# A two-part transformer block on one core: query-score chunks moved up behind the key-score chunks of the same number

## The reference, cut to what matters

```python
scores = jnp.einsum('bqhd,bkhd->bhqk', Qh, Kh) / np.sqrt(dh)
scores = jnp.where(key_mask[:, None, None, :] == 0, NEG, scores)
scores = jnp.where(tril[None, None, :, :] == 0, NEG, scores)
attn = jax.nn.softmax(scores, axis=-1)
attn = attn * query_mask[:, None, :, None]
out = jnp.einsum('bhqk,bkhd->bqhd', attn, Vh).reshape(B, T, U)
out = out + x            # and a layer norm with gamma and beta behind it
```

## Time and profile before

| what | value |
|---|---|
| runs | 536.09, 537.47, 538.89 us; median 537.47 |
| profiled execution | 538.71 us, its span 536.9 us |
| mean granted clock of PE over the span | 0.942 |
| busy shares of the span | PE 83%, DVE 76%, ACT 59%, POOL 23% |
| attention stage, first key chunk | from 209.15 us |

### The profile page before, as it was taken

One profiled execution on the slowest core, in us unless ns is written; L12 is line 12 of the kernel. 1 busy time (PEld: TensorE's weight loads), 2 busy tenths in 40 slices (PEclk: granted clock), 3 DMA queues, 4 the chain that ended last, 5 costly groups with the idle time before them and its releaser, 6 DMA issues.

```text
span 536.9 us, 10757 instructions
## 1 busy us (share of the span) xinstructions
PE 447.4 (83%) x3773; PEld 275.3 (51%) x3773; DVE 406.4 (76%) x1008; ACT 315.3 (59%) x670; POOL 124.7 (23%) x345
## 2 busy tenths in 40 slices
PE   0049545988999739999999999999999999999981
PEld 0026334766777515565555555555556556556540
DVE  6898988887884238576977877877878878887715
ACT  0029135977888803566656666656667567566670
POOL 8000000000000011001045045045054063072181
PEclk9999958989999955799999999999999999999997
DMA  8900021223333351122122222322212213212000
GB/s 220 295 20 0 20 80 43 75 80 98 98 98 88 110 146 22 47 76 62 56 83 67 72 67 66 85 56 66 85 53 77 82 46 93 64 48 69 2 21 20
DMA packets 28585, 39.68 MB, mean 74 GB/s; under 512 B 5751, under 2 KB 19959, under 8 KB 28535
## 3 DMA queue, kind: packets, MB, share of 16 engines
q1 hardware_dynamic: 28486, 39.03, 26.0%
q10 hardware_dynamic: 48, 0.01, 0.0%
HBM read 25.91 MB, written 10.49 MB: 68 GB/s over the span
## 4 chain that ended last, share of the span: by engine, by line
PE 55%; DVE 6%; issue 1%; ACT 1%; DVEq 0%; ACTq 0%
PE banks L979 15%; PE banks L1010 14%; PE banks L998 13%; PE banks L981 6%; PE banks L1000 5%; DVE mx L837 3%; PE banks L1020 3%; DVE stats L879 1%; DVE aggr L883 1%; ACT pt L950 0%; ACT ots L934 0%; PE banks L988 0%; DVE res L866 0%; DVE res L869 0%; DVE mixed L870 0%
## 5 line engine op out<-in xcount | busy, mean ns | idle before, releaser
L837 DVE TENSOR_REDUCE mx<-banks 128x1 f32<-128x384 f32 (+3 forms) x384 | 212.5, 598 | 59.7 <-PE banks L981 52.5
L950 ACT ACTIVATE pt<-banks 128x512 f32<-128x512 f32 (+2 forms) x384 | 184.8, 528 | 110.4 <-PE banks L1000 104.1
L981 PE MATMUL banks<-causal,ident_b 128*128 128x128 bf16 x512 | 106.8, 228 | 0.0
L1000 PE MATMUL banks<-causalT,ident_b 128*128 128x128 bf16 x512 | 103.7, 222 | 0.0
L979 PE MATMUL banks<-w_room 73*128 73x512 bf16 (+3 forms) x256 | 75.3, 331 | 11.5 <-DVEq L912 10.3
L1010 PE MATMUL banks<-pt,vg 128*9 128x512 f32 (+3 forms) x1024 | 81.9, 438 | 0.5 <-ACT pt L950 0.5
L998 PE MATMUL banks<-w_room 76*128 76x512 bf16 (+3 forms) x256 | 71.2, 310 | 0.0
L979 PE MATMUL banks<-k_odd,q_odd 73*128 73x512 bf16 (+3 forms) x256 | 69.0, 302 | 1.6 <-DVE mx L837 1.6
L998 PE MATMUL banks<-q_odd,k_odd 76*128 76x512 bf16 (+3 forms) x256 | 67.6, 300 | 2.0 <-ACT pt L950 2.0
L750 POOL TENSOR_SCALAR mneg<-mx 128x16 f32<-128x16 f32 x32 | 8.1, 253 | 197.9 <-DVEq L845 197.9
L981 PEld LDWEIGHTS banks<-causal,ident_b 128*128 128x128 bf16 x512 | 52.1, 102 | 0.0
(11 more groups left out here) (155 smaller groups left out, 615.7 us busy)
## 6 DMA issues: line engine op xcount, KB each, us to landing
k_scratch<-parts SPq DMA_DIRECT2D x40, 128.0 KB, 2.3
w_room<-q_scratch SPq DMA_DIRECT2D x48, 96.0 KB
w_room<-k_scratch SPq DMA_DIRECT2D x48, 96.0 KB
q_odd<-q_scratch SPq DMA_DIRECT2D x48, 96.0 KB
k_odd<-k_scratch SPq DMA_DIRECT2D x48, 96.0 KB
q_scratch<-parts SPq DMA_DIRECT2D x24, 128.0 KB, 2.3
w_room<-in_w_dram SPq DMA_DIRECT2D x1, 2048.0 KB, 9.2
xn_all<-xn_st SPq DMA_DIRECT2D x8, 256.0 KB, 2.4
```

What stands on the lines that cost most here:

```text
L837: ins = dve.tensor_reduce(mx[:, u % 2, heads[0]:heads[-1] + 1, q], banks[:, S0 + c % RING, 0:w * len(heads)].rearrange("p (h k) -> p h k", ...
L950: act.activation(weights(k, heads[0], len(heads)), banks[:, ST0 + j % RING, 0:(T - P * k) * len(heads)], ACT.Exp, scale=SCALE).then_inc(ex ...
L981: ins = mm(o[:, w - P:w], ident_b[:, :], causal[:, :], start=False, stop=True)
L1000: ins = mm(o[:, 0:P], ident_b[:, :], causalT[:, :], start=False, stop=True)
```

## The change

Query chunk number j now stands directly behind key chunk number j, for all j. The short run of products V23 stands behind S2, not between K2 and S1, and the long run V01 stands behind S10, not ahead of it. The wait for the loads of the group g + 2 stays ahead of S0, so it now stands directly behind K0.

```diff
                         for j in range(NCH):
                             keys(tok, par, g, j)
+                            if ahead:
+                                if first and (g, j) == (2, 0):
+                                    pe.wait_ge(ones_in[1], 32)
+                                if j == 0:
+                                    loaded = stack_in[par if g + 2 < NG else 1 - par][(g + 2) % NG]
+                                    pe.wait_ge(loaded, tok.next(loaded, UNIT_DMAS))
+                                chunk(tok, par, g + 2, j)
                             if behind and j == 2:
                                 values(prev, 2)
                                 values(prev, 3)
                             if j == 10:
                                 values(g, 0)
                                 values(g, 1)
-                            for c in ((), (0,), (1,), (2, 3))[j] if j < 4 else (j,):
-                                if not ahead:
-                                    break
-                                if first and (g, c) == (2, 0):
-                                    pe.wait_ge(ones_in[1], 32)
-                                if c == 0:
-                                    loaded = stack_in[par if g + 2 < NG else 1 - par][(g + 2) % NG]
-                                    pe.wait_ge(loaded, tok.next(loaded, UNIT_DMAS))
-                                chunk(tok, par, g + 2, c)
                             if j == 3 and not (last and g == NG - 1):
                                 maxima(tok, g + 1)
```

## The result

The changed kernel takes 542.98 us in the median of five runs (541.76 to 543.19), the kernel before 536.78 us in five runs (536.09 to 538.89; the 537.47 from which the forecast started is the median of the first three). The ratio of the runs is 1.0096, 95% interval 1.0078 to 1.0114: about 1% or 5 us slower. The two medians alone are 6.2 us apart, 1.2%, a little more than that interval holds. The forecast was 543.1.

What follows compares the result with a forecast made beforehand. Bound: PE's own 9.40 us per plain group plus about 0.27 us of waits, ScalarE's 2.50 us run setting K7. Terms +6.1 - 0.4 = +5.7 us on the 537.47 median: 543.2, taken as 543.1; 8-in-10 range 540.0 to 546.5.

Steps and rivals of the forecast that it cites:

- (1): Query chunk S10 moved ahead of the long run V01: only moves VectorE's idle time, worth 0.
- (2): Ahead of K3: one more 512-column chunk, 2.53 us instead of 2.25, so K3 and ScalarE's run come 0.28 us later.
- (3): K3 to K7: ScalarE's 2.50 us stand, PE waits about 0.54 us, K7 at K0 + 5.03 instead of 4.75.
- (4): VectorE in plain groups: S6's 0.14 us wait goes, worth 0; group 9.95 us, +0.28 us 22 times, +6.1 us.
- (5): Groups where VectorE also makes the previous batch's statistics: 10.09 us instead of 10.15, -0.06 us 7 times, -0.4 us.
- (6): First group, at PE's low clock: PE's own work exceeds ScalarE's run, so 0, at most +0.1 us; last two groups 0.
- (7): Other engines' waits (copy L934, mask row, loads): all covered; uncovered, each would cost at most 0.28 us per group.
- Rival A: K7's 0.12 us wait comes from VectorE's delay of S6; PE's waits vanish, plain groups 9.40, 531.1 us; 6%.
- Rival B: K4's exponential is tied to transpose MX, not K3, so K7 stays at K0 + 4.75; no change, 537.1 us; 5%.
- Rival C: ScalarE's 0.25 us idle ahead of K4's exponential waits for K4, so K7 can follow K3 by 2.25; 537.8 us; 4%.
- Rival D: PE's clock grant falls in the regular 0.54 us wait, one group per batch at least 3.8 us longer; 573 us; 2%.
- Rival E: ScalarE's occasional delays come more often or a cover is missing: up to another 0.28 us per group, 549 us; 4%.

Runs made afterwards that it cites:

- the last experiment: Changed kernel with statistics moved, maxima copy behind K4's exponential, attended-rows copy behind K5's, OUT and its use one chunk later: 525.69 us, ratio 0.9793.

## Why the prediction was right, point by point

- What bounds: 9.40 us of PE's own work and two waits, one of them ScalarE's. Right; the last experiment measures 9.41, and the first two measures of K3 to K7, in the earlier trace rows, already said which wait was the floor.
- (1) S10 is worth 0: ratio 1.000 (0.9987 to 1.0014) alone.
- (2) K3 at K0 + 2.53: 2.52. MX at 3.08: 3.08.
- (3) PE waits 0.55 us ahead of K7 (0.54 expected) and K7 stands at 5.03: 327.17 less 322.14. The mechanism follows ScalarE's run one to one over three lengths.
- (4) VectorE waits less, S6 waits no more, and it is worth 0: so it is. The walk for VectorE had S0 to S2 at 0.76, 1.37 and 1.98 and S3 at 3.28; the row has three in one stretch from 0.87, and the fourth at 3.28. The start was missed by 0.11 us because S11 is reduced right ahead of S0 and the program waits there for its own reduction: 0.24 us idle, the same 0.24 that in most statistics groups stands ahead of L879, where the profile names the reduction itself. Nothing hung on it. A plain group was to be 9.95 and is 9.94 to 9.95, in 22 groups +0.27 each, 6.0 us against 6.1.
- (5) The groups with statistics: 10.07 to 10.08 against 10.15 in six of them, -0.07 where -0.06 was expected. The seventh was not at 10.15 as the prediction had it, but at 10.42: VectorE's statistics start about 0.35 us late there in both kernels, S1 is ready in time in both, and it stays at 10.42. Six times -0.07 is the -0.4 us all the same.
- (6) The first group was put at 0 to 0.1 and came out at +0.43. This term was mis-sized. K7 and K8 of it are at the same distance from K0 (6.93 or 6.94, and 7.79) in both kernels; what differs is when within V01 the clock is granted in full. By the granted clock of stretches of 0.5 us, 0.95 in 222.00 to 222.50 before and 0.77 in 221.00 to 221.50 after, the grant rose from 0.50 to 1.00 about 12.9 us behind K0 before and 13.8 after; an estimate from these is 0.9 us longer at half speed, 0.44 us, which is the whole +0.43. Over the profiles of the experiments that group took 13.86 to 15.14 us, both ends in the new order, and 14.16 to 14.64 in the kernels in which K3 stands as before. So this term varies by more than its shift here; what sets the moment of the rise was not looked into, and that stays open.
- (7) The other waits stayed covered: no wait of PE for L934, for the mask row or for a load stands in the changed kernel's steady part.
- Rival A, waits vanish with nothing in their place: K3 to K7 stayed at 2.51, and it took more edits, in ScalarE's, VectorE's and PE's programs, to get there. Rival B, the exponential tied to MX: MX stood still and the exponential moved by 0.27 us with K3. Rival C: refuted by K3 to K7 at 2.51 with K4 0.62 behind K3. Rival D, the clock: the grant stayed at 1.00,

```profile
229.00:500.00 271.00, 260.55 (x2746) 155.86 (x2747) 210.77 (x480) 176.78 (x381) 92.55 (x270) 1.00 0.25 67
```

  with 0.55 us of waiting in each plain group, so the case that the Trainium skill describes in "TensorE: Matmul & The Clock Gate", section "A second HAM failure mode: psum-queue depth-cycling", did not occur. Rival E: the late exponential of the earlier trace rows came again exactly once.
- The 543.1 against 542.98: that the two agree to 0.1 us is luck. The forecast added +5.7 us to a median of 537.47; the next runs of the kernel before brought that median to 536.78. Step by step the traces give -1.71 us in the untouched stage, +0.43 in the first group, which was put at nothing, and +5.54 in the 29 groups. The last number is the one that the prediction's steps (1) to (5) stand or fall by, and it is 0.2 us below their +5.7.

The estimate from the Trainium skill, "ScalarE: Activation LUTs", section "What ACT_TABLE_LOAD costs", would have had the run 0.23 us shorter. In the earlier trace rows neighbouring activations of 512 elements overlap by 0.11 us (0.60 long, 0.49 apart), near the page's 93 ns; the missing part is the 0.25 us that the program waits for its own copy.

## What to carry to other kernels

Before moving work on the busiest engine, find the instruction behind which another engine does several things in a row, and look how far the first user of the last of them stands: here K3 to K7. Such a run is read off best where the busy engine has nothing else to do, as in the last group but one, where the same 2.51 us stood beside an idle PE. VectorE, helped at a place where ScalarE held PE longer, gave nothing. And when two engines squeeze the same place, look at both before choosing an order: with ScalarE's long run the new order lost 6 us, with the run shortened the two were equal, each with a wait of its own, and the fastest version uses the new order, in which VectorE's wait is gone. Which order is better depends on which wait can still be taken away; that the old one would be slower in the end was not run.

## What was not expected of the hardware

Two delays come back at the same place of the program in the kernel before and in the changed one: the exponential of K4 0.29 us late in the third group of the fourth batch, and the statistics 0.35 us late in the third batch. For the first, ScalarE idles 0.54 us behind the maxima copy in the earlier trace rows; its timeline in the same group of the changed kernel:

```profile
356.08 0.26 ACT L926 ACTIVATE mT<-banks 48x128 bf16<-48x128 bf16 x1
356.88 1.64 ACT L950 ACTIVATE pt<-banks 128x384 f32<-128x384 f32 x4 [0.54 <-PE banks L1000]
```

In all other groups of these two kernels it idles 0.23 to 0.25 us there. Over the twelve profiles the delay is not always in that place: seven have it in this group (0.47 to 0.57 us idle; the fastest version, whose group is 9.70 us instead of 9.41, among them), the one with the copy made twice has it in another group, the last of the second batch (0.53 us), and the four with only the copy L934 moved, with or without the statistics, have it in none. The late statistics stand in the third batch in all nine kernels in which the statistics were not moved. So each delay sits at a wait of an engine for its own instruction, and came back in the same group wherever that engine's program was unchanged. In the kernel before the two cost about 0.6 us together. What they are was not tried.
